# GpSimd's scatters spread out and tied to a tile's finish, and the last ranking one beat sooner, in a cross-attention block with a routed feed-forward layer

## The chip, the cores and the metric

One core of one Trainium2 chip. Its engines are TensorE (PE), VectorE (DVE), ScalarE (ACT), GpSimd (POOL) and SyncE (SP, which here only starts transfers). The metric is the device time of one launch in microseconds (us); lower is better.

## The reference, cut to what matters

`x` has 16 batches of 256 rows of 128 features, `ctx` 16 batches of 64 rows. All is float32.

```python
x = x + tanh(g_xattn) * xattn(layernorm(x), ctx)      # 16 heads of 8, masked softmax
h = layernorm(x)
top1 = argmax(softmax(h @ router_w + router_b))       # one of E = 8 experts per row
for i in range(E):
    hh = h @ w1[i] + b1[i]                            # 128 -> 2 * 512
    a, g = split(hh, 2)
    y = (a * sigmoid(g)) @ w2[i] + b2[i]              # 512 -> 128
    out = out + where(top1 == i, y, 0)
x = x + tanh(g_ffn) * out
```

## The kernel before, in words

Everything is written out by hand, engine by engine: each engine has a fixed list of instructions and waits on semaphores for the others. Nothing is reordered by a scheduler.

**The attention stage** runs over the batches b = 0 to 15 (two row tiles of 128 rows each, so 32 row tiles in all). In step i TensorE makes the scores of batch i + 1 while ScalarE takes the exponentials of batch i. TensorE turns the row shifts of a batch (`shifts`, L1299), ScalarE copies them to SBUF (L653), TensorE adds them to the scores (L1221), and only then can the exponentials (L621) start. GpSimd adds the output bias to a batch's rows (`add_bias`, L403), copies queries (`queries`, L409), and works out the scale and shift of the second layer norm (`rstd_2`, L427 to L432), which ScalarE applies (`norm2`, L630).

**Routing.** A row's expert is chosen on VectorE (`choose`, L900 to L913) in six groups of batches. TensorE counts the rows that come before each row of the same expert (`ranks`, L1283 and L1287), VectorE turns this into a row number in a DRAM buffer (`place`, L924 to L932; `pos` is the result), and GpSimd scatters each row tile of 128 rows (its normalized form, its residual and its index, 1056 bytes a row) into the buffer `routed_rows` with an indirect DMA (`scatter`, L416). There are 32 scatters. The first 22 (`ET`) are enough for a first table of 14 (`T1`) expert tiles; the last ten (22 to 31) belong to batches 11 to 15. GpSimd does the first 22 in the attention steps, as many in a step as `room` allows: those of group 3 (18 to 21) in step 14.

**The expert stage** runs over `FT` = 39 tiles of 128 routed rows. For tile t: SP fetches the rows (`fetch`, L340), TensorE turns them (`turn`, L1387), ScalarE copies the result (`rows`, L697), TensorE multiplies with the expert's first matrix (`up`, L1403; the even tiles go to `ps_A`, the odd ones to `ps_B`), ScalarE takes the sigmoid (`gates_of`, L704), VectorE multiplies (`gate`, L1043), TensorE multiplies with the second matrix (`down`, L1418), VectorE adds the residual (`finish`, L1054, which raises `fo_ready`), and GpSimd scatters the tile to the output (`store`, L486). Before that GpSimd has added the second bias to the fetched rows (`residual`, L480). VectorE and ScalarE also copy the next expert's weights (`weights`, L1033 and L690). TensorE's order in a beat is `up(t + 1)`, `turn(t + 2)`, `down(t)`.

The first 14 tiles run from the first table. Meanwhile the rest of the routing is done: VectorE chooses the last group after `finish(3)`, TensorE ranks it in beat 5, VectorE places it after `finish(5)`, SP writes a block of padding rows behind each expert's region (eight DRAM-to-DRAM transfers of 132 KB, L352), GpSimd sends scatters 22 to 25 in the first beats and 26 to 31 in beats 6 to 10, and VectorE makes the second table in three pieces (`tiles_left`, `second_table`, `second_rows`, L1004 to L1021) after `finish(6)`, `finish(7)` and `finish(8)`. SP fetches tile 14 only when all scatters and padding have landed and the second table is there.

## Time and profile before

| | us |
|---|---|
| median of 3 runs | 280.49 (278.85 to 280.64) |
| the profiled execution | 280.14 |
| its span, first to last instruction | 278.0 |

| engine | busy | share of the span |
|---|---|---|
| TensorE, matmuls | 245.6 | 88% |
| VectorE | 209.0 | 75% |
| GpSimd | 158.5 | 57% |
| ScalarE | 156.7 | 56% |

TensorE has 80% of the chain of work that ended last. The profiled execution lies 0.35 us under the median, and 2.14 us of it lie outside the span. Times below are counted from the start of the span. In the rows, "idle before <- releaser" is the time in which the engine did nothing before that instruction, and what ended it; "remote" and "another core or an unknown queue" stand where the profile finds no event that fits the release.

### The profile page before, as it was taken

To read this page: it belongs to the slowest core of one execution; us is meant where nothing else is said; L and a number is where in the kernel's file an instruction comes from. 1 tells how busy PE (TensorE), PEld (TensorE's weight loads), DVE (VectorE), ACT (ScalarE), POOL (GpSimd) and SP (SyncE) were. 2 spreads that over 40 slices of the span, in tenths; PEclk is the share of its full clock that TensorE was granted. 3 is DMA by queue.
4 is the path that set the end of the run, shared out by engine and by line. 5 is a ranking of instruction groups with operands and counts; after the bars stand their busy time and mean duration, and the time that the engine had idled before them with its cause. 6 is when DMAs were issued, how large, how long until landed. Compare 5 with 4: busy or idle time off the path is not lost.

```text
span 278.0 us, 8458 instructions
## 1 busy us (share of the span) xinstructions
PE 245.6 (88%) x2411; PEld 184.2 (66%) x2411; DVE 209.0 (75%) x608; ACT 156.7 (56%) x436; POOL 158.5 (57%) x254
## 2 busy tenths in 40 slices
PE   3979999999999989989599899399979999999950
PEld 2554445555555555544248899299979999999940
DVE  6988998898989879879649489276757777776720
ACT  5487978777566566545086765256434444444410
POOL 6505426259677585384833775826863645577740
PEclk9999999999999999999989999889999999999995
DMA  6999930000111010021244401535442222100000
GB/s 177 258 298 368 348 114 4 2 1 2 41 40 41 22 60 23 19 80 41 78 103 136 119 28 44 175 90 138 119 111 66 64 84 58 47 21 22 22 5 0
DMA packets 22412, 24.13 MB, mean 87 GB/s; under 512 B 3728, under 2 KB 19539, under 8 KB 22241
## 3 DMA queue, kind: packets, MB, share of 16 engines
q1 hardware_dynamic: 18880, 17.05, 21.7%
q0 software_dynamic: 2784, 6.43, 6.5%
q8 instruction: 21, 0.34, 0.5%
q10 hardware_dynamic: 704, 0.13, 0.2%
q14 instruction: 23, 0.18, 0.2%
HBM read 16.23 MB, written 8.91 MB: 90 GB/s over the span
## 4 chain that ended last, share of the span: by engine, by line
PE 80%; ACT 5%; issue 5%; another core or an unknown queue 3%; DVE 2%; POOL 2%; ACTq 1%; POOLq 0%
PE ps_B L1403 12%; PE ps_A L1403 12%; PE ps_O L1238 11%; PE ps_O L1418 6%; PE ps_B L1204 5%; PE ps_Y L1418 5%; PE ps_A L1176 4%; PE ps_Y L1249 3%; PE ps_B L1269 3%; PE ps_B L1212 3%; PE ps_B L1163 2%; PE ps_A L1181 2%; PE ps_B L1221 2%; PE ps_B L1140 1%
## 5 line engine op out<-in xcount | busy, mean ns | idle before, releaser
L486 POOL DMA_INDIRECT out_dram<-sb_early,sb_k x39 | 39.3, 1008 | 32.8 <-DVE sb_early L1054 30.2
L416 POOL DMA_INDIRECT routed_rows<-sb_xr,sb_pos x32 | 33.1, 1034 | 25.1 <-DVE sb_pos L932 9.2
L1403 PE MATMUL ps_B<-sb_early 128*128 128x128 f32 x304 | 38.8, 282 | 7.4 <-ACT sb_early L697 7.3
L870 DVE TENSOR_REDUCE sb_shift<-ps_A 128x16 bf16<-128x1024 f32 x32 | 39.0, 1218 | 6.3 <-PE ps_A L1181 5.7
L1403 PEld LDWEIGHTS ps_B<-sb_early 128*128 128x128 f32 x304 | 36.8, 198 | 8.1 <-ACT sb_early L697 8.1
L1403 PE MATMUL ps_A<-sb_early 128*128 128x128 f32 x320 | 39.1, 275 | 0.4 <-ACT sb_early L697 0.4
L621 ACT ACTIVATE sb_pT<-ps_B 128x512 f32<-128x512 f32 x64 | 33.0, 603 | 10.0 <-PE ps_B L1221 10.0
L1403 PEld LDWEIGHTS ps_A<-sb_early 128*128 128x128 f32 x320 | 37.3, 192 | 0.7 <-ACT sb_early L697 0.7
L1043 DVE SCALAR_TENSOR_TENSOR sb_qT<-ps_A,sb_b1T,sb_qT 128x128 f32<-128x128 f32 x80 | 22.5, 344 | 19.9 <-ACT sb_qT L704 12.6
L704 ACT ACTIVATE sb_qT<-ps_A,sb_b1T 128x128 f32<-128x128 f32 x80 | 22.8, 367 | 24.9 <-PE ps_A L1403 22.5
L704 ACT ACTIVATE sb_qT<-ps_B,sb_b1T 128x128 f32<-128x128 f32 x76 | 21.8, 368 | 23.7 <-PE ps_B L1403 21.1
L1043 DVE SCALAR_TENSOR_TENSOR sb_qT<-ps_B,sb_b1T,sb_qT 128x128 f32<-128x128 f32 x76 | 21.4, 344 | 14.7 <-ACT sb_qT L704 12.3
L859 DVE RECIPROCAL sb_inv<-ps_O 128x128 f32<-128x128 f32 x32 | 30.3, 946 | 1.8 <-PE ps_O L1238 1.7
L480 POOL TENSOR_TENSOR sb_k<-sb_k,sb_b_g 128x128 f32<-128x128 f32 x39 | 25.7, 660 | 8.7 <-DMA sb_k<-routed_rows 6.7
L1033 DVE COPY sb_early<-sb_w 128x1024 f32 (+1 forms) x39 | 24.8, 637 | 2.5 <-issue 2.5
L1418 PE MATMUL ps_O<-sb_w,sb_qT 128*128 x160 | 21.2, 276 | 0.0
L630 ACT ACTIVATE sb_xr<-sb_xr,sb_nmr,sb_rstd 128x128 f32<-128x128 f32 x32 | 14.1, 487 | 12.0 <-POOL sb_nmr L432 12.0
L1418 PE MATMUL ps_Y<-sb_w,sb_qT 128*128 x152 | 20.3, 277 | 0.0
L1418 PEld LDWEIGHTS ps_O<-sb_w,sb_qT 128*128 128x128 f32 x160 | 19.4, 192 | 0.0
L1204 PE MATMUL ps_B<-sb_qT,sb_k 32*128 32x256 f32 x256 | 18.3, 400 | 1.0 <-issue 1.0
L1418 PEld LDWEIGHTS ps_Y<-sb_w,sb_qT 128*128 128x128 f32 x152 | 18.5, 192 | 0.0
L427 POOL TENSOR_SCALAR sb_neg<-sb_mv 128x2 f32<-128x2 f32 x16 | 3.8, 234 | 25.4 <-DVE sb_mv L891 22.9
(183 smaller groups left out, 464.1 us busy)
## 6 DMA issues: line engine op xcount, KB each, us to landing
sb_k<-routed_rows SPq DMA_DIRECT2D x39, 132.0 KB, 2.0
sb_w<-in_L_ffn_w_dram SPq DMA_DIRECT2D x4, 1024.0 KB, 11.2
sb_w<-in_L_ffn_w_dram SPq DMA_DIRECT2D x4, 512.0 KB, 10.2
sb_xr<-in_x_dram SPq DMA_DIRECT2D x3, 512.0 KB, 7.0
routed_rows<-routed_rows SPq DMA_DIRECT2D x8, 132.0 KB
routed_rows<-sb_pad_rows SPq DMA_DIRECT2D x7, 132.0 KB, 5.7
out_dram<-sb_early,sb_k POOLq DMA_INDIRECT x39, 2.5
sb_ctx_sb<-in_ctx_dram SPq DMA_DIRECT2D x2, 256.0 KB, 4.0
```

The source lines that it names most:

```text
L416: pool.indirect_dma_start(routed[:, :], bass.IndirectOffsetOnAxis(ap=pos[:, t:t + 1], axis=0), xr[:, t, :], None, bounds_check=ROWS - 1, o ...
L480: pool.tensor_tensor(fr[:, k, 0:D], fr[:, k, 0:D], b2_g[:, bass.ds(e, 1), :].rearrange("p o d -> p (o d)"), ALU.add).then_inc(res_ready, 1)
L486: pool.indirect_dma_start(out_rows, bass.IndirectOffsetOnAxis(ap=fr[:, k, 2 * D:2 * D + 1].bitcast(I32), axis=0), fo[:, k, :], None, bound ...
L621: act.activation(pT[:, g, :, :].rearrange("p a s -> p (a s)"), psB[g][:, :], ACT.Exp, scale=SCALE)\
L704: act.activation(sig[:, k, f * P:(f + 1) * P], gate_bank(k)[:, f * P:(f + 1) * P], ACT.Sigmoid, bias=b1T[:, bass.ds(e, 1), FB + f:FB + f + ...
L859: dve.reciprocal(inv[:, q], psO[:, S + t * P:S + (t + 1) * P]).then_inc(inv_ready, 1)
L870: dve.tensor_reduce(shift_parts[:, t, :, 0:HG], psA[:, :].rearrange("p (g h k) -> p g h k", g=G, k=C), AX.X, ALU.max).then_inc(a_max, 1)
L1043: dve.scalar_tensor_tensor(out=hid[:, k, f * P:(f + 1) * P], in0=up_bank(k)[:, f * P:(f + 1) * P], scalar=b1T[:, bass.ds(e, 1), f:f + 1].r ...
L1204: pe.matmul(psB[g][:, k * S:(k + 1) * S], k4[r, b, 2 * k:2 * k + 2, :].rearrange("p h k -> p (h k)"), qT[r, b, :], start=(k == 0), stop=Fa ...
L1238: last = pe.matmul(psO[SLOT * g:SLOT * g + SLOT, c * S:(c + 1) * S], kept, pT[:, g, k, :], start=(k == 0), stop=(k == 1), tile_position=(0 ...
L1403: last = pe.matmul((up_bank, gate_bank)[c](k)[:, f * P:(f + 1) * P], w_1s[:, k, o:o + P], fxT[:, k, :], start=True, stop=True)
L1418: last = pe.matmul((psO, psY)[k][:, 0:D], hid[:, k, f * P:(f + 1) * P], w_2[:, bass.ds(e, 1), f:f + 1, :], start=(f == 0), stop=(f == FB - 1))
```

## The change

1. GpSimd, attention steps: in a step that may scatter several tiles, the first one (the first two in step 14) goes out, then come the bias addition and the copy of queries, and then the other scatters. Before, all scatters came first. In step 14 `rstd_2` moves behind all of it.
2. GpSimd, expert stage: each beat t > 0 now waits for `finish(t - 1)` ahead of its scatter or store. The six late scatters (26 to 31) go out one a beat in beats 5 to 10; before, two in beat 6 and one in each of beats 7 to 10, with no wait for a finish. The stores of tiles 4 and on come correspondingly later.
3. VectorE: the expert numbers of tiles 1 and 2 are read from the table after the first weight copies and not ahead of them; the last `place` stands after `finish(4)`, the pieces of the second table after `finish(5)`, `finish(6)` and `finish(7)`.
4. TensorE: the last `ranks` stands after `down(4)`, ahead of `up(6)`; before, after `turn(7)`.

```diff
@@ GpSimd, attention steps @@
+                for k in range(2 if i == B - 2 else 1):
+                    if sent < ready and room:
+                        scatter(sent)
+                        sent += 1
+                        room -= 1
+                if i in RSTD_AT:
+                    rstd(RSTD_AT[i])
+                if has(i + 1):
+                    add_bias(i + 1)
+                if streamed(i + 3):
+                    queries(i + 3)
                 while sent < ready and room:
                     scatter(sent)
                     sent += 1
                     room -= 1
                 if i == B - 2:
                     rstd_2(i - 1)
-                if i in RSTD_AT:
-                    rstd(RSTD_AT[i])
-                if has(i + 1):
-                    add_bias(i + 1)
-                if streamed(i + 3):
-                    queries(i + 3)
@@ GpSimd, expert stage @@
                 if t + 2 < FT:
                     residual(t + 2)
+                if t > 0:
+                    pool.wait_ge(fo_ready[(t - 1) % NR], (t - 1) // NR + 1)
                 if t == 0:
                     scatter(ET + 2)
                     scatter(ET + 3)
-                elif 6 <= t < 11:
-                    for k in range(2 if t == 6 else 1):
-                        scatter(late)
-                        late += 1
+                elif 5 <= t < 11:
+                    scatter(late)
+                    late += 1
                 else:
                     store(kept)
@@ VectorE @@
-            e_0, e_1, e_2 = expert(0), expert(1), expert(2)
+            e_0 = expert(0)
             weights(0, e_0)
             choose(LAST_GROUP - 1)
+            e_1 = expert(1)
             weights(1, e_1)
             invert(B - 1)
             place(LAST_GROUP - 1)
             gate(0, e_0)
+            e_2 = expert(2)
             weights(2, e_2)
...
-                if t == 5:
+                if t == 4:
                     place(LAST_GROUP)
                     dve.wait_ge(region_ready, LAST_GROUP + 1)
                     dve.tensor_copy(pad_i[:, :], region0[0:1, :]).then_inc(pad_ready, 1)
+                if t == 5:
+                    tiles_left()
                 if t == 6:
-                    tiles_left()
+                    second_table()
                 if t == 7:
-                    second_table()
-                if t == 8:
                     second_rows()
                     dve.wait_ge(table_ready, 2)
@@ TensorE @@
-                if t == 5:
-                    ranks(LAST_GROUP)
                 if t == T1:
                     pe.wait_ge(table_ready, 2)
                 down(t)
+                if t == 4:
+                    ranks(LAST_GROUP)
```

GpSimd's list in attention steps 13 and 14 (L416 are scatters 16 to 21, L403 the bias additions, L427 and on `rstd_2`). Before:

```order
L416 DMA routed_rows<-sb_xr,sb_pos 34688x264 x2
L403 TENSOR_TENSOR sb_xr<-sb_xr,sb_bo_g 128x2x128
L416 DMA routed_rows<-sb_xr,sb_pos 34688x264 x4
L427 TENSOR_SCALAR sb_neg<-sb_mv 128x2
L428 TENSOR_SCALAR sb_ve<-sb_mv 128x2
```

and now:

```order
L416 DMA routed_rows<-sb_xr,sb_pos 34688x264
L403 TENSOR_TENSOR sb_xr<-sb_xr,sb_bo_g 128x2x128
L416 DMA routed_rows<-sb_xr,sb_pos 34688x264 x3
L403 TENSOR_TENSOR sb_xr<-sb_xr,sb_bo_g 128x2x128
L416 DMA routed_rows<-sb_xr,sb_pos 34688x264 x2
L427 TENSOR_SCALAR sb_neg<-sb_mv 128x2
```

The four scatters of step 14 have a bias addition in their middle, and `rstd_2` stands behind that addition as well.

GpSimd's list in the expert stage where the late scatters begin (L480, now L485, is `residual`, L486, now L491, is `store`). Before, from the store of tile 4 on:

```order
L486 DMA out_dram<-sb_early,sb_k 4096x128 [waits fo_ready4]
...
L480 ISA [waits row_in8]
L480 TENSOR_TENSOR sb_k<-sb_k,sb_b_g 128x128
L416 DMA routed_rows<-sb_xr,sb_pos 34688x264 [waits h_ready,pos_ready] x2
...
L480 ISA [waits row_in9]
L480 TENSOR_TENSOR sb_k<-sb_k,sb_b_g 128x128
L416 DMA routed_rows<-sb_xr,sb_pos 34688x264 [waits h_ready,pos_ready]
```

and now, from the store of tile 3 on:

```order
L491 DMA out_dram<-sb_early,sb_k 4096x128 [waits fo_ready3]
...
L485 ISA [waits row_in7]
L485 TENSOR_TENSOR sb_k<-sb_k,sb_b_g 128x128
L416 DMA routed_rows<-sb_xr,sb_pos 34688x264 [waits h_ready,pos_ready,fo_ready4]
...
L485 ISA [waits row_in8]
L485 TENSOR_TENSOR sb_k<-sb_k,sb_b_g 128x128
L416 DMA routed_rows<-sb_xr,sb_pos 34688x264 [waits h_ready,pos_ready,fo_ready5]
```

The scatters begin one beat earlier, each has a wait for a tile's finish, and the pair is gone.

TensorE's list around the last ranking. Before:

```order
L1418 MATMUL ps_O<-sb_w,sb_qT 128x128
L1403 MATMUL ps_A<-sb_early 128x128 [waits w1_act,hid_ready,w1_ready,fx_ready]
L1403 MATMUL ps_A<-sb_early 128x128 x7
L1387 MATMUL ps_B<-sb_ident,sb_k 128x128 [waits fx_ready,row_in7]
L1283 MATMUL ps_B<-sb_onehot,sb_before 128x48 [waits p_ready,lg_ready,region_ready,onehot_ready]
L1287 MATMUL ps_B<-sb_onehot,sb_ones_b 128x48
```

and now (L1426 is `down`, L1291 and L1295 `ranks`, L1411 `up`, L1395 `turn`):

```order
L1426 MATMUL ps_O<-sb_w,sb_qT 128x128
L1291 MATMUL ps_B<-sb_onehot,sb_before 128x48 [waits p_ready,lg_ready,region_ready,onehot_ready]
L1295 MATMUL ps_B<-sb_onehot,sb_ones_b 128x48
...
L1411 MATMUL ps_A<-sb_early 128x128 [waits w1_act,hid_ready,w1_ready,fx_ready]
L1411 MATMUL ps_A<-sb_early 128x128 x7
L1395 MATMUL ps_B<-sb_ident,sb_k 128x128 [waits fx_ready,row_in7]
```

The ranking stands one `up` and one `turn` earlier.

## Rows read from the trace of the kernel before

**Rows 1.** The chain that ended last, in time: start, us, what; `up(6)`, `up(18)`, `up(38)`.

```profile
166.18 1.79 PE ps_A L1403 x16
...
208.08 1.79 PE ps_A L1403 x16
...
263.86 1.79 PE ps_A L1403 x16
```

**Rows 2.** Timeline, 132 to 138: start, us, engine, line [idle before <- releaser].

```profile
131.99 1.00 POOL L416 DMA_INDIRECT routed_rows<-sb_xr,sb_pos  x1 [2.58 <-DVE sb_pos L932]
...
135.84 0.97 POOL L416 DMA_INDIRECT routed_rows<-sb_xr,sb_pos  x1 [0.31 <-issue]
...
134.84 0.29 PE L1299 MATMUL ps_Y<-sb_identb,sb_shift 128*128 128x128 bf16 x2
...
137.73 0.38 ACT L653 ACTIVATE sb_sm<-ps_Y 128x256 bf16<-128x256 bf16 x1 [4.61 <-remote]
```

**Rows 3.** Timeline, 171 to 180, GpSimd, TensorE, ScalarE and VectorE.

```profile
171.56 1.00 POOL L416 DMA_INDIRECT routed_rows<-sb_xr,sb_pos  x1 [1.15 <-DVE sb_pos L932]
...
179.47 1.00 POOL L416 DMA_INDIRECT routed_rows<-sb_xr,sb_pos  x1 [0.17 <-issue]
...
173.64 0.27 PE L1387 MATMUL ps_B<-sb_ident,sb_k 128*128 128x128 f32 x1
...
179.62 3.39 PE L1403 MATMUL ps_B<-sb_early 128*128 128x128 f32 x16 [4.81 <-ACT sb_early L697]
...
179.29 0.28 ACT L697 ACTIVATE sb_early<-ps_B 128x128 f32<-128x128 f32 x1 [3.38 <-remote]
...
179.43 1.12 DVE L1043 SCALAR_TENSOR_TENSOR sb_qT<-ps_A,sb_b1T,sb_qT 128x128 f32<-128x128 f32 x4 [5.07 <-remote]
```

**Rows 4.** Timeline, 189 to 205, GpSimd, TensorE and ScalarE.

```profile
189.77 0.99 POOL L486 DMA_INDIRECT out_dram<-sb_early,sb_k  x1 [0.30 <-issue]
...
203.37 0.99 POOL L486 DMA_INDIRECT out_dram<-sb_early,sb_k  x1 [0.17 <-issue]
...
202.38 0.27 PE L1387 MATMUL ps_B<-sb_ident,sb_k 128*128 128x128 f32 x1
...
204.69 0.28 ACT L697 ACTIVATE sb_early<-ps_B 128x128 f32<-128x128 f32 x1 [0.99 <-remote]
```

**Rows 5.** SP's issues (start, us from first to last issue), its wait for the table, tile 14's rows on GpSimd.

```profile
139.32 15.96 SPq L340 DMA_DIRECT2D sb_k<-routed_rows  x14
171.62 11.83 SPq L352 DMA_DIRECT2D routed_rows<-routed_rows  x8
186.82 27.65 SPq L340 DMA_DIRECT2D sb_k<-routed_rows  x17
...
SPq L356 <- DVE sb_tile_row L1021: 2.5, 1, 2.5
...
189.03 0.45 POOL L480 TENSOR_TENSOR sb_k<-sb_k,sb_b_g 128x128 f32<-128x128 f32 x1 [6.68 <-DMA sb_k<-routed_rows]
```

**Rows 6.** Timeline, 117 to 121: three scatters in a row, and the shifts of batch 13.

```profile
117.99 1.12 POOL L416 DMA_INDIRECT routed_rows<-sb_xr,sb_pos  x1 [1.55 <-ACT sb_xr L630]
...
118.91 0.28 PE L1299 MATMUL ps_Y<-sb_identb,sb_shift 128*128 128x128 bf16 x2
...
119.32 0.38 ACT L653 ACTIVATE sb_sm<-ps_Y 128x256 bf16<-128x256 bf16 x1 [1.96 <-PE ps_Y L1299]
```

**Rows 7.** Timeline, 138 to 144: the end of `rstd_2(13)`, `norm2(13)`, the first weight copy.

```profile
138.30 0.19 POOL L432 TENSOR_TENSOR sb_nmr<-sb_neg,sb_rstd 128x2 f32<-128x2 f32 x1
...
140.80 0.90 ACT L630 ACTIVATE sb_xr<-sb_xr,sb_nmr,sb_rstd 128x128 f32<-128x128 f32 x2
...
143.72 0.43 DVE L1033 COPY sb_early<-sb_w 128x512 f32 x1 [2.46 <-issue]
```

**Rows 8.** Timeline, 264, VectorE: `finish(36)`.

```profile
264.05 0.34 DVE L1054 SCALAR_TENSOR_TENSOR sb_early<-ps_O,sb_tanh_g,sb_k 128x128 f32<-128x128 f32 x1
```

**Rows 9.** Timeline, 169 to 171, VectorE: the last placing.

```profile
169.98 0.21 DVE L924 TENSOR_TENSOR sb_slot<-ps_B,sb_region 128x48 f32<-128x48 f32 x1
```

## The prediction

> **What bounds the kernel now.** I read the chain of work that ended last, first by engine: TensorE has 80% of it. The same chain in order of time gives the pace of the expert stage. From `up(18)` to `up(38)` it takes 263.86 - 208.08 = 55.78 us for 20 tiles, so 2.79 us a tile with TensorE never idle; the time of a tile there can't be beaten by anything GpSimd does. From `up(6)` to `up(18)` it takes 41.90 us for 12 tiles, where the pace asks for 33.47 [rows 1]. So 8.4 us are lost there. Then I looked in the timelines of the single engines for the place of this loss and for others like it. There are three holes, and each has the same look: TensorE has done its work, the engine that waits for its signal gets it late, and the profile names no releaser.
>
> - First: TensorE turns the shifts of batch 15 at 134.84, 0.29 us long. ScalarE copies them at 137.73, after 4.61 us idle, "remote" [rows 2]. Late by 137.73 - 135.13 = 2.6 us.
> - Second: `turn(9)` ends at 173.91, ScalarE's copy of it starts at 179.29; VectorE's gate starts at 179.43, after 5.07 us idle, also "remote". TensorE waits 4.81 us, and the next `up` takes 3.39 us [rows 3] against 1.79 at full clock [rows 1]: 1.6 us more. Together 6.4 us.
> - Third: `turn(17)` ends at 202.65, its copy starts at 204.69 [rows 4]: late by 2.0, of which the tile loses 1.7, since a normal copy waits a little as well. 6.4 + 1.7 = 8.1, which with the ranking of about 0.2 us in beat 5 accounts for the 8.4.
>
> What they have in common is GpSimd. In the first it sends four indirect DMAs in one row, 1.28 us apart (131.99 to 135.84) [rows 2]. In the second six scatters in 7.9 us, 171.56 to 179.47 [rows 3], while SP sends its eight padding blocks (171.62 on) [rows 5]. In the third nine stores in 13.6 us, 1.7 us apart [rows 4], while SP fetches. The counterparts: with only two scatters out (117.99 and one more of the row of three) the signal of the shifts is late by 119.32 - 119.19 = 0.13 us [rows 6], and where there is one store to each 2.79 us, in the 20 tiles from 208.08 on, nothing is late at all [rows 1]. I take it that TensorE's signals are held up while GpSimd's indirect DMAs come closer than about 2 us for several in a row. The trace shows this together, not as cause and effect.
>
> **Part 1, the scatters of the attention steps.** In step 14 the four scatters get `add_bias` between the second and the third. At 134.84 to 135.13, when TensorE's signal of batch 15 goes out, the third has just begun now; then only two are out, and the addition (about 0.75 us) runs. The nearest case is that of [rows 6], 0.13 us late. I take the hold as gone: ScalarE's copy comes 2.6 us sooner, and with it the exponentials of batch 15. But `norm2(13)`, next on ScalarE at 140.80, needs `rstd_2(13)`. That ends at 138.30 + 0.19 = 138.49 now, and with the addition ahead of it at 138.49 + 0.75 = 139.24. So ScalarE gains only 140.80 - 139.24 = 1.6 us; behind that it is ScalarE's row (`norm2(13)`, weights, table load, `norm2(14)`, the first copy of rows) that lets the expert stage begin. The gain lies between 0 (the hold stays) and 2.6 us (ScalarE catches up the rest from its short waits for TensorE); I take 1.6. If the hold stays, the 0.75 us are hidden: 139.24 is before 140.80. The first scatter of the second pair goes 0.75 us later, so SP's first fetch goes from 139.32 to 140.1, and with the 2.2 us of a fetch (186.82 issued, used at 189.03 [rows 5]) the rows are there at 142.3. The first `turn` is some 2 us behind that. The other steps (6, 9, 12, 13) only swap an addition or a copy that nobody waits for with a scatter: nothing.
>
> **Part 2, the wait for `finish(t - 1)`.** The wait makes one indirect DMA a beat, 2.79 us apart, the spacing that is free of holds. Behind it on GpSimd stand the scatter or store and `residual(t + 3)`; the latter is needed by `finish(t + 3)`, three beats on, and takes 0.45 us [rows 5], so its cover is some 7 us. The stores start later by up to four tiles, and the buffers (14 of them) are refilled late: the store of tile 4 comes in beat 11, and SP fetches tile 18 behind it, some five beats before TensorE turns it. So I cost it at nothing. The second and third holds go in full: 8.1 us. From below: if the padding blocks hold TensorE by themselves, up to 6.4 of it stays.
>
> What is late next is tile 14. Its fetch waits for three things. Now it is the second table that comes last: SP waits 2.5 us for it, and issues at 186.82 [rows 5]. In the new order the table is done a beat sooner and the padding begins sooner (part 3). The last scatter, though, is bound to `finish(9)`. In steady beats a finish starts 0.2 us behind the beginning of the next beat but one's `up` (`finish(36)` at 264.05 [rows 8], `up(38)` at 263.86 [rows 1]). So, counted from the start of `up(11)`, `finish(9)` starts at +0.2, and `turn(14)`, two beats and one `up` of 1.79 us later, at +7.4. The scatter can start some 0.15 us behind the finish, at +0.2 + 0.34 + 0.15 = +0.7. From the last scatter before the first table to SP's first fetch it was 139.32 - 135.84 = 3.48 us [rows 2, 5], which gives +4.2, and the rows are there 2.2 us later, at +6.4. Slack 1.0 us: covered, but not by much. A landing 2 us slower costs 1.0 us, once.
>
> GpSimd's scatters took their 1.00 us in the second hold, with VectorE copying weights in the same beats [rows 3]. The Trainium skill ("SBUF — State Buffer", SBUF: two separate sides) says that GpSimd cannot write the descriptors of its DMAs while VectorE runs a float32 copy from SBUF to SBUF, and gives 3.1 us instead of 0.62 for a DMA in such a collision. The rows don't show such a price; by it the last scatter, released by VectorE's own finish, would be up to 2.5 us late and tile 14 would cost 1.5 us, so 272.2 in place of 270.7.
>
> **Part 3, the last group and the table a beat sooner.** The same instructions on VectorE and TensorE, only moved. `place` starts at 169.98 now, behind `finish(5)` [rows 9]; behind `finish(4)`, which ends near 168.1, it starts 1.9 us sooner. It takes 0.9 us and pushes `gate(6)` and the weights of tile 8 back by that, of which TensorE has near 1.9 us in hand: nothing. TensorE's ranking is 0.2 us in either place. SP's padding starts at some 169.8 in place of 171.62, and its 11.83 us with the landing end near 184, before the last scatter's end. The expert numbers of tiles 1 and 2 leave VectorE's way ahead of the first copy, which now waits 2.46 us for three of them [rows 7]; two thirds, 1.6 us, are gained for VectorE, but the expert stage starts on ScalarE's chain. I take nothing, at most 0.5 us.
>
> **The sum**, against the profiled execution: span 278.0 - 1.6 - 8.1 = 268.3; with the 2.14 us outside the span 270.4; with the 0.35 us by which the profiled execution lies under the median 270.8, rounded to 270.7.
>
> **Rivals.**
>
> 1. The padding is the cause of the second hold. For it: the hold begins 2 us after SP's first padding DMA, and after only two scatters, fewer than in the first hold. Against it: the padding goes on until 183.45, and the signals come at 179.3 [rows 3, 5]. Then 3.2 to 6.4 us stay: 273.9 to 277.1.
> 2. The first hold stays, since four scatters in 5.9 us are still dense: 270.7 + 1.6 = 272.3.
> 3. The holds have nothing to do with GpSimd, but with the place in the program (each engine loading its next piece of code, say), and the change does not do what it is for: 280.5, or 1 us to either side. Against it: in 20 tiles at the spaced pace nothing of the kind shows [rows 1]. The Trainium skill ("Runtime: NRT & Kernel Launch", Instruction fetch mechanics) says that the sequencers stream their code ahead in 16 KiB blocks, mostly hidden; by that such a hold would be rare, which speaks against this rival too.
> 4. Slower: the holds stay, and the fetch of tile 14 now hangs on the last scatter. A hold amid the beats moves `finish(9)` and `turn(14)` alike, so the slack stays 1.0 us. If the last scatter lands 4 us later than I take (held up in its turn), TensorE waits 3.0 us at tile 14 and restarts at the slow clock (1.6 us more, as in the second hold): 280.5 + 4.6 = 285.1; a landing 2.5 us late gives 282.0. It decides from a lateness of 1.0 us. Against it: today's fetches and the first group's scatters landed in the usual time amid dense traffic.
>
> **How the numbers follow.** All three holds go: 0.42, 269.5 to 271.5. Rival 2: 0.14. Rival 1, in part or in full: 0.25. Rival 3: 0.14. Rival 4: 0.05. Faster by over 1% means under 277.7: the forecast, rival 2 and rival 1, together 0.81. Within 1%, which is about what a measurement of this kernel can tell from no change: 0.14. Slower: 0.05. The range that leaves out no more than 2 in 10 reaches from 268 (the 2.6 us of part 1 in full and 0.5 of part 3) to 277.6 (rival 1 in full).
>
> **What would show it.** In the changed kernel's timeline: ScalarE's copy of batch 15's shifts within 0.3 us of TensorE's turn; no "remote" of over 1 us; late scatters 2.8 us apart; TensorE's beats at 2.79 us from tile 8 to 18; `norm2(13)` released by GpSimd; tile 14's rows there within 1 us of its turn. I am wrong if a hold of several microseconds stays while the scatters are spaced (then it is the padding or the place), or if TensorE waits for the fetch of tile 14.

## The result, and the profile after

| | median | lowest to highest | runs |
|---|---|---|---|
| before | 280.65 us | 278.85 to 281.96 | 6 |
| after | 276.71 us | 275.52 to 277.38 | 6 |

The ratio is 0.986, 95% interval 0.982 to 0.990: faster by 1.4%, 3.9 us. The forecast was 270.7, 9.8 us faster. Here and below, executions with a lower granted clock and a time over 1.5% above the kernel's fastest are left out; there are two such of w1 and two of v1. The profiled execution of the changed kernel took 276.95 us, its span is 275.2 us, its mean granted clock 0.989 (before: 278.0 us and 0.976). Line numbers have moved: `up` is L1411 now, `turn` L1395, `down` L1426, ScalarE's gates L710 and its copy of the turned rows L703, VectorE's gate L1049, the store L491, the scatter L416.

First the chain of work that ended last, in order of time (start, us, what), for the pace of `up`: `up(0)`, `up(6)`, `up(13)`, `up(14)`, `up(16)` to `up(20)`, `up(38)`.

```profile
144.57 2.05 PE ps_A L1411 x16
...
164.70 1.89 PE ps_A L1411 x16
...
184.32 1.80 PE ps_B L1411 x16
187.80 1.79 PE ps_A L1411 x16
...
193.38 1.79 PE ps_A L1411 x16
196.85 2.05 PE ps_B L1411 x16
199.90 1.79 PE ps_A L1411 x16
202.69 1.79 PE ps_B L1411 x16
206.29 2.05 PE ps_A L1411 x16
...
261.05 1.79 PE ps_A L1411 x16
```

A "hold" is, as in the prediction, a stretch in which TensorE's signal is late. From `up(6)` to `up(13)` it is 19.62 us for seven tiles, 2.80 a tile: the second hold [rows 3] is gone, and so is the third [rows 4] as one piece. From `up(13)` to `up(14)` it is 3.48 us, 0.69 too much. Then something new: `up(16)` to `up(17)` takes 3.47, `up(17)` to `up(18)` 3.05, the next 2.79, then 3.60 to `up(20)`. Three tiles take 206.29 - 196.85 = 9.44 us where the pace asks for 8.37: 1.07 too much. The same pattern comes six times, with the slow `up` at 196.85, 206.29, 215.75, 225.20, 234.63 and 244.05: 6.4 us in all. Before, from 208.08 on, no tile lost anything [rows 1].

GpSimd's timeline around two of these places (start, us, engine, line; in brackets the idle time before and its releaser):

```profile
189.25 0.99 POOL L491 DMA_INDIRECT out_dram<-sb_early,sb_k  x1 [0.75 <-DVE sb_early L1060]
...
192.51 0.99 POOL L491 DMA_INDIRECT out_dram<-sb_early,sb_k  x1 [1.77 <-DVE sb_early L1060]
193.81 1.28 POOL L491 DMA_INDIRECT out_dram<-sb_early,sb_k  x1 [0.30 <-issue]
...
195.74 0.99 POOL L491 DMA_INDIRECT out_dram<-sb_early,sb_k  x1 [0.17 <-issue]
...
198.88 0.99 POOL L491 DMA_INDIRECT out_dram<-sb_early,sb_k  x1 [1.65 <-DVE sb_early L1060]
```

and ScalarE's gates of the same tiles:

```profile
191.63 1.14 ACT L710 ACTIVATE sb_qT<-ps_B,sb_b1T 128x128 f32<-128x128 f32 x4 [1.48 <-PE ps_B L1411]
...
195.48 1.14 ACT L710 ACTIVATE sb_qT<-ps_A,sb_b1T 128x128 f32<-128x128 f32 x4 [2.54 <-PE ps_A L1411]
```

The reader is to see that the stores are one a beat, except where a second one follows at once (192.51 and 193.81, then 195.74). That is the kernel's catch-up: in each third beat `if t % 3 == 2 and ... kept < t` sends a second store. In that beat ScalarE's gate waits 2.54 us in place of 1.48. It starts 1.06 us later after the start of its `up` than in the beats beside it, 0.39 us after the pair's second store ends (195.09) and before the third starts. Behind the gate stands ScalarE's copy of the next tile's rows (196.50, 0.29 us), and the next `up` starts when it is done, at 196.85. That `up` takes 2.05 us in place of 1.79; the granted clock is 1.00 from 194 to 200, so this is not the clock. A group so loses some 0.8 us by the late start of the `up` and 0.26 by its length.

In the kernel before, the stores ran free, and the backlog was gone at 207. But its timeline has such a pair too, in the beat that the same rule picks:

```profile
200.36 0.99 POOL L486 DMA_INDIRECT out_dram<-sb_early,sb_k  x1 [0.16 <-issue]
201.65 1.06 POOL L486 DMA_INDIRECT out_dram<-sb_early,sb_k  x1 [0.30 <-issue]
```

The third hold begins there. ScalarE's gate of that beat, at 202.56, waited 2.24 us, and the copy of rows came 2.04 us after its turn [rows 4]. The six stores before this pair, from 189.77 to 198.24 and 1.6 to 2.0 us apart, made no gate wait over 1.48 us. So the third hold was itself a pair of this rule, and the change turned one into six.

The first hold moved and shrank. Scatters started at 131.27, 132.55, 134.45 and 135.75, with the addition between the second and the third. ScalarE copied the shifts of batch 15 at 136.51, released by TensorE, not 137.73 after a "remote" wait [rows 2]. But VectorE's reciprocal ahead of it started late:

```profile
134.03 0.96 DVE L865 RECIPROCAL sb_inv<-ps_O 128x128 f32<-128x128 f32 x1 [2.25 <-remote]
```

TensorE's products for it ended at 132.38, between the first two scatters (131.27 to 132.25 and 132.55 to 133.53), and VectorE starts on them at 134.03, 0.5 us after the second has ended. TensorE waited 1.46 us ahead of batch 15's scores, before 0.32. So a pair makes a hold in this stage too.

`up(0)` came at 144.57, before at 146.52: 1.95 us gained, 1.6 forecast.

### The profile page after: what moved, and what is told of

Same layout as the page of the kernel before. It is cut to its first block, busy times and chain, and to the rows that moved or that the text cites. A ratio compares the mean times of both kernels' runs of the same rounds, so it can differ in the third digit from the quotient of the medians.

```text
span 275.2 us, 8490 instructions
## 1 busy us (share of the span) xinstructions
PE 245.3 (89%) x2411; PEld 183.3 (67%) x2411; DVE 208.8 (76%) x608; ACT 156.5 (57%) x436; POOL 153.3 (56%) x254
## 4 chain that ended last, share of the span: by engine, by line
PE 79%; issue 6%; DVE 4%; ACT 3%; DMA 2%; POOL 1%; ACTq 0%; SPq 0%; POOLq 0%; DVEq 0%
PE ps_A L1411 13%; PE ps_B L1411 12%; PE ps_O L1246 10%; PE ps_O L1426 6%; PE ps_Y L1426 6%; PE ps_B L1212 6%; PE ps_A L1184 3%; PE ps_B L1277 3%; PE ps_B L1220 3%; PE ps_Y L1257 3%; PE ps_B L1171 2%; PE ps_A L1189 2%; PE ps_B L1229 2%; DMA sb_xr<-in_x_dram 2%; ACT sb_pT L627 2%
## 5 line engine op out<-in xcount | busy, mean ns | idle before, releaser
L491 POOL DMA_INDIRECT out_dram<-sb_early,sb_k x39 | 39.6, 1015 | 37.0 <-DVE sb_early L1060 31.1
L416 POOL DMA_INDIRECT routed_rows<-sb_xr,sb_pos x32 | 33.3, 1039 | 27.2 <-ACT sb_xr L636 7.5
L1411 PE MATMUL ps_A<-sb_early 128*128 128x128 f32 x320 | 39.5, 277 | 2.8 <-issue 2.4
L1411 PE MATMUL ps_B<-sb_early 128*128 128x128 f32 x304 | 37.6, 277 | 3.4 <-issue 2.6
L1411 PEld LDWEIGHTS ps_A<-sb_early 128*128 128x128 f32 x320 | 37.3, 192 | 3.7 <-issue 3.0
L1411 PEld LDWEIGHTS ps_B<-sb_early 128*128 128x128 f32 x304 | 35.4, 192 | 4.5 <-issue 3.3
L710 ACT ACTIVATE sb_qT<-ps_A,sb_b1T 128x128 f32<-128x128 f32 x80 | 22.8, 368 | 26.9 <-PE ps_A L1411 26.9
L710 ACT ACTIVATE sb_qT<-ps_B,sb_b1T 128x128 f32<-128x128 f32 x76 | 21.8, 369 | 26.5 <-PE ps_B L1411 25.8
L1049 DVE SCALAR_TENSOR_TENSOR sb_qT<-ps_A,sb_b1T,sb_qT 128x128 f32<-128x128 f32 x80 | 22.5, 345 | 17.6 <-ACT sb_qT L710 13.1
L1049 DVE SCALAR_TENSOR_TENSOR sb_qT<-ps_B,sb_b1T,sb_qT 128x128 f32<-128x128 f32 x76 | 21.4, 345 | 15.9 <-ACT sb_qT L710 8.1
L485 POOL TENSOR_TENSOR sb_k<-sb_k,sb_b_g 128x128 f32<-128x128 f32 x39 | 19.9, 511 | 4.5 <-DMA sb_k<-routed_rows 2.4
L1426 PE MATMUL ps_O<-sb_w,sb_qT 128*128 x160 | 21.3, 276 | 0.4 <-DVE sb_qT L1049 0.4
L1426 PE MATMUL ps_Y<-sb_w,sb_qT 128*128 x152 | 20.2, 276 | 0.0
L1426 PEld LDWEIGHTS ps_O<-sb_w,sb_qT 128*128 128x128 f32 x160 | 19.4, 192 | 0.7 <-issue 0.7
L1426 PEld LDWEIGHTS ps_Y<-sb_w,sb_qT 128*128 128x128 f32 x152 | 18.5, 192 | 0.0
L427 POOL TENSOR_SCALAR sb_neg<-sb_mv 128x2 f32<-128x2 f32 x16 | 3.7, 234 | 25.0 <-DVE sb_mv L897 23.2
```

The costliest lines, as they stand in the source:

```text
L416: pool.indirect_dma_start(routed[:, :], bass.IndirectOffsetOnAxis(ap=pos[:, t:t + 1], axis=0), xr[:, t, :], None, bounds_check=ROWS - 1, o ...
L491: pool.indirect_dma_start(out_rows, bass.IndirectOffsetOnAxis(ap=fr[:, k, 2 * D:2 * D + 1].bitcast(I32), axis=0), fo[:, k, :], None, bound ...
L710: act.activation(sig[:, k, f * P:(f + 1) * P], gate_bank(k)[:, f * P:(f + 1) * P], ACT.Sigmoid, bias=b1T[:, bass.ds(e, 1), FB + f:FB + f + ...
L1049: dve.scalar_tensor_tensor(out=hid[:, k, f * P:(f + 1) * P], in0=up_bank(k)[:, f * P:(f + 1) * P], scalar=b1T[:, bass.ds(e, 1), f:f + 1].r ...
L1411: last = pe.matmul((up_bank, gate_bank)[c](k)[:, f * P:(f + 1) * P], w_1s[:, k, o:o + P], fxT[:, k, :], start=True, stop=True)
L1426: last = pe.matmul((psO, psY)[k][:, 0:D], hid[:, k, f * P:(f + 1) * P], w_2[:, bass.ds(e, 1), f:f + 1, :], start=(f == 0), stop=(f == FB - 1))
```

## The experiments

Eighteen runs on five chips, called B to F here; A is the chip of the result, which the record doesn't name. Each ran beside the kernel before on its own chip. The kernel before itself has a trace on A and C alone; elsewhere the last column goes by the traces of the kernels that ran there.

| chip | kernel before there | runs of before | holds in the traces |
|---|---|---|---|
| A | 280.65 | 6 | yes |
| B | 268.34 | 25 | none |
| C | 268.88 | 29 | none |
| D | 268.38 | 18 | none |
| E | 283.47 | 7 | yes |
| F | 282.86 | 7 | yes |

So the first finding was not asked for: the same kernel takes 268 us on B, C and D and 281 to 283 on A, E and F. B to F were used on one occasion each, so the chip and what else went on at that time can't be told apart. Ratios below are to the kernel before on the same chip, with their 95% interval.

### Chip B

**x1_no_pairs.** The changed kernel without the second store of each third beat; what is left over is stored after the last tile.

```diff
-                    if t % 3 == 2 and t > 11 and kept < t:
-                        store(kept)
-                        kept += 1
-            store(FT - 1)
+            while kept < FT:
+                store(kept)
+                kept += 1
```

> The changed kernel with never two stores in one beat; the nine stores that it is behind go out in a row after the last tile. Pair theory (TensorE's signals are held when two indirect DMAs follow each other 1.3 us apart and a third soon after): every beat from tile 18 to 38 is 2.79 us, up(18) to up(38) takes 55.8 us and not the 62.2 of the changed kernel, and no TensorE signal is over 0.3 us late; the whole time is about 270.5 plus 9 to 12 us of stores at the end, so 279 to 283. Rival (the lateness belongs to the place in the program, or to the wait for a finish): the beats of tiles 20, 23, 26, 29, 32 and 35 stay about 1.07 us longer.

Measured: 276.10 us (two executions), ratio 1.025 (1.016 to 1.034). With no hold there is nothing to save, and the leftover shows: seven stores (not nine, as expected) after the last paced one at 256.70, 1.28 us apart, the last at 265.62. The catch-up can't simply be dropped.

**x2_addition_in_pair.** The changed kernel with one of the additions that GpSimd makes anyway (`residual`) put between the two stores of a pair.

```diff
+                    if added < FT:
+                        residual(added)
+                        added += 1
                     store(kept)
```

> The changed kernel with the next tile's residual addition between the two stores of a pair, so that they start 1.65 us apart and not 1.3. If it is the missing gap between two indirect DMAs: the six late beats go, 276.7 - 6.4 = 270.3. If it is three indirect DMAs within 3.3 us whatever stands between: 276 to 277, as the changed kernel.

Measured: 270.35 us, ratio 1.004 (1.000 to 1.008). That this is the 270.3 of the expectation is an accident: the chip has no holds that could have gone. Nor is the spacing the 1.65 us that was meant. In the trace the stores start at 192.29, 194.50 and 195.79: the addition parts the two stores of the beat, and is then missing ahead of the next beat's store, which follows 1.29 us behind. The pair is moved.

**x3_stores_unpaced.** The changed kernel with the wait for `finish(t - 1)` only in beats 1 to 10: `if 0 < t < 11:`.

> The changed kernel without the wait for a finish from beat 11 on; the late scatters stay paced. Pair theory: GpSimd catches up in one stretch after tile 14's rows are there (nine stores 1.65 us apart), which costs one hold of 0 to 2.5 us as before, and from then on one store a beat and no late beats: 270.5 to 273. If the lateness belongs to the number of stores that are caught up, whenever: 276 to 277.

Measured: 270.42 us, ratio 1.003 (0.999 to 1.007).

**x4_before_scatters_paced.** The kernel before, with that wait in beats 7 to 10 alone, so that four of the late scatters come one a beat.

```diff
+                if 6 < t < 11:
+                    pool.wait_ge(fo_ready[(t - 1) % NR], (t - 1) // NR + 1)
```

> The kernel before with one edit: the late scatters of beats 7 to 10 wait for the finish of the tile before (the pair in beat 6 stays). If the crowd of scatters is the cause of the 6.4 us hold at tile 9: 280.65 - 6.4 to 280.65 - 4.5 = 274.2 to 276.2. If the eight padding blocks are: the hold stays, 280 to 281.

Measured: 269.38 us, ratio 1.002 (0.999 to 1.006). The pair of scatters in beat 6 stays. None of the four says anything of the holds, since chip B has none.

### Chip C

**y1_before_again.** The kernel before, unchanged, for its trace on another chip.

> The kernel before, unchanged, for its trace on the chip of this batch. In the first four experiments the kernel before took 268.3 us beside them, and 280.65 beside the changed kernel. If the holds of TensorE's signals are a matter of the chip or of what runs beside it: where it takes near 268 its trace has no signal over 0.3 us late, where it takes 280 it has the three holds.

Measured: 269.4 us, span 267.2, granted clock 0.983. Its timeline at the place of the second hold, GpSimd, then ScalarE:

```profile
170.13 0.98 POOL L416 DMA_INDIRECT routed_rows<-sb_xr,sb_pos  x1 [0.30 <-issue]
...
171.77 1.00 POOL L416 DMA_INDIRECT routed_rows<-sb_xr,sb_pos  x1 [0.17 <-issue]
...
173.71 1.00 POOL L416 DMA_INDIRECT routed_rows<-sb_xr,sb_pos  x1 [0.16 <-issue]
...
175.37 1.27 POOL L416 DMA_INDIRECT routed_rows<-sb_xr,sb_pos  x1 [0.17 <-issue]
...
175.91 1.14 ACT L704 ACTIVATE sb_qT<-ps_A,sb_b1T 128x128 f32<-128x128 f32 x4 [0.63 <-PE ps_A L1403]
...
178.69 1.14 ACT L704 ACTIVATE sb_qT<-ps_B,sb_b1T 128x128 f32<-128x128 f32 x4 [0.62 <-PE ps_B L1403]
```

The six scatters come in 8.5 us (168.83 to 177.31), in [rows 3] in 7.9, and ScalarE's gates start 0.6 us after it is free, 2.8 us apart, with no "remote". `up(0)` starts at 143.78 and `up(38)` at 253.12; on chip A it was 146.52 and 263.86 [rows 1]. The differences, 2.7 and then 8.0 more, are close to the first hold's 2.6 and the 8.1 of the other two, as the prediction had sized them. For the other two this is good evidence, from one trace on each chip. For the first it is in part luck: on C the granted clock was 0.52 from 129 to 132, on A 1.00, so the two stages differ in more than the hold.

TensorE's signals were also on time amid scatters 1.3 us apart. The first group's scatters start at 130.32, 131.63, 132.91 and 134.19, TensorE's work ends at 132.93 and at 133.47, and VectorE and ScalarE start on it at 133.00 and 133.51.

**y2_after_again.** The changed kernel, unchanged.

> The changed kernel, unchanged, beside the kernel before on the chip of this batch. Pair theory as it was: 268.3 x 0.986 = 264.5. If the holds are absent on this chip (kernel before near 268): no hold to save, so the change is worth its other parts alone, 267 to 270. On a chip with holds (kernel before near 280): 276 to 277.5.

Measured: 269.69 us, ratio 1.001 (0.998 to 1.004). The pairs of stores are there and cost nothing. Only the step to tile 14 is long: `up(13)` at 184.01, `up(14)` at 187.61, 0.81 us too much.

**y3_scatter_order_alone.** The kernel before with part 1 of the change (the order in the attention steps) and nothing else.

> The kernel before with the new order of scatters and additions in the attention steps alone. Without holds on the chip: the kernel before's time within 0.3%. With holds: the first hold goes or shrinks, 1 to 2 us less than the kernel before.

Measured: 270.39 us, ratio 1.005 (1.003 to 1.008), a little over the 0.3% of the expectation. The executions of the kernel before fall in two groups here, 267.7 to 268.9 and 269.5 to 271.2; the ten of this run, 269.8 to 270.8, all lie in the upper one. Differences of half a per cent on the chips without holds may be no more than this.

**y4_after_unpaced.** The changed kernel with no wait for `finish(t - 1)` at all.

> The changed kernel with no wait for a finish at all; the ranking, placing, table and scatters stand where the change put them. Without holds on the chip: within 0.3% of the changed kernel, or faster by what the pace holds up. With holds: the crowd of late scatters is back, 278 to 281.

Measured: 269.49 us, ratio 1.001 (0.998 to 1.004). GpSimd's stores from 187.73 to 205.91 are twelve, 1.65 us apart in the mean (the first two 1.30), and the chain has TensorE at its full pace beside them (5.58 us for two tiles):

```profile
197.32 1.79 PE ps_A L1409 x16
...
202.90 1.79 PE ps_A L1409 x16
```

### Chip D

**z1_part3_alone.** The kernel before with what the prediction calls part 3 (the ranking, the placing and the table a beat sooner), and with the late scatters one a beat from beat 5 but no wait for a finish; attention steps and free-running stores as before.

> The kernel before with part 3 alone: the late scatters from beat 5, one a beat, the last ranking, placing and table a beat sooner, the expert numbers of tiles 1 and 2 later; order of the attention steps and free-running stores as before. Where no hold shows in the trace of the kernel before: this is worth nothing, ratio 1.000 within 0.004. If instead the scatters one a beat by program order do the work of the wait where holds exist (kernel before near 280 us), the second hold is gone or halved here, 274 to 277 us; if the pacing by the wait is what counts, GpSimd still runs ahead and the second hold stays, 279 to 281.

Measured: 269.76 us, ratio 1.003 (1.000 to 1.005): part 3 is worth nothing here, as forecast.

**z2_last_scatters_looser.** The changed kernel, with a looser wait in beats 7 to 10.

```diff
                 if t > 0:
-                    pool.wait_ge(fo_ready[(t - 1) % NR], (t - 1) // NR + 1)
+                    u = t - 1 if t < 7 or t > 10 else t - 2
+                    pool.wait_ge(fo_ready[u % NR], u // NR + 1)
```

> The changed kernel, with the wait of beats 7 to 10 for the finish of two tiles back in place of one, so that the last late scatter goes a beat sooner and with it the fetch of tile 14. Theory: the 0.7 to 0.8 us that TensorE loses between tile 13 and tile 14 come from the fetch that hangs on that scatter, and go: 0.7 us less than the changed kernel on the same chip, the step from tile 13 to 14 at 2.79 us. Rival: they come from VectorE's queue (its gate late for another reason), and the step stays 3.5 us.

Measured: 269.46 us, ratio 1.005 (1.004 to 1.007). The chain shows `up(12)` at 180.76 and `up(14)` at 186.34, which is 5.58 for two tiles: the delay of tile 14 is gone, so it came from the fetch behind the last scatter. The changed kernel was not run on this chip, so the 0.7 us of the expectation can't be seen in the time; the ratio to the kernel before, 1.005, shows no gain.

**z3_addition_in_pair_again** and **z4_before_scatters_paced_again** are x2 and x4 once more.

> The changed kernel with an addition between the two stores of a pair. If this chip shows holds (kernel before near 280 us): the theory that a pair of stores 1.3 us apart delays TensorE's signal by 1.1 us, once in three tiles, six times, gives 276.7 - 6.4 = 270.3, or 273.5 if the addition spaces them only half enough; the rival (the delay of each third tile has to do with something else) gives 276.7. Without holds: 1.00 of the kernel before.

> The kernel before with a wait for the finish of the tile before in beats 7 to 10 alone. If this chip shows holds (kernel before near 280 us): the theory of crowded scatters takes the second hold away, up to 6.4 us, so 274 to 276 us, with the first and the third hold left; the rival (padding or place in the program) leaves it at 280. Without holds: 1.00 of the kernel before.

Measured: 270.34 us, ratio 1.008 (1.007 to 1.010), and 270.82, ratio 1.007 (1.003 to 1.010); 1.00 was expected of both without holds. No holds on D either.

### Chip E

**w1_bursts_of_four.** The changed kernel with its stores from tile 11 to 35 in bursts.

```diff
+                elif t < 11 or t >= 36:
+                    if kept < t:
+                        store(kept)
+                        kept += 1
+                elif t % 4 == 3:
+                    for k in range(5 if t < 20 else 4):
+                        if kept < t:
+                            store(kept)
+                            kept += 1
```

> The changed kernel with its stores in bursts from tile 11 to 35: four (at first five) in a row each fourth beat, none in the beats between, no denser row of indirect DMAs exists in any of the kernels. Theory: a row of indirect DMAs some 1.3 us apart delays TensorE's signals by itself, on any chip, if only it is long enough: then six bursts, each with a hold of 2 to 5 us as in the kernel before on the first chip, 12 us or more over the changed kernel, and 'remote' waits in the trace. Rival: on this chip nothing of the kind happens whatever the spacing; the time is that of the changed kernel within 1 us, up to 2 us more if the additions behind a burst come late to finish.

Measured: 294.15 and 297.88 us, beside 283.47 for the kernel before: 11 to 14 us slower. In the kernel before on chip A there were two holds in the expert stage [rows 3, 4]. Here the list of waits (us in total, times, longest) has:

```profile
DVE sb_qT L1054 <- remote: 32.0, 8, 5.4
ACT sb_early L708 <- remote: 13.0, 7, 3.2
ACT sb_qT L715 <- remote: 6.6, 2, 3.3
```

**w2_spaced_and_looser.** x2 and z2 together in one kernel.

> The changed kernel with an addition between the two stores of a pair and with the late scatters waiting for the finish of two tiles back. If this chip shows holds (kernel before near 280 us): the pair theory and the tile 14 repair give 276.7 - 6.4 - 0.7 = 269.6; the rival (the lengthened third tiles are no matter of pairs) gives 276.0. Without holds: as the kernel before within 0.5 per cent.

Measured: 274.25 us, ratio 0.965 (0.958 to 0.972): the fastest version on a chip with holds, 9.2 us under the kernel before.

**w3_before_scatters_paced_third.** x4 again, here with holds.

> The kernel before with a wait for the finish of the tile before in beats 7 to 10 alone. With holds on this chip (kernel before near 280 us): the theory of crowded scatters gives 274 to 276, the rival (padding or place in the program) 280. Without holds: 1.00 of the kernel before.

Measured: 278.59 us, ratio 0.982 (0.977 to 0.987), 4.9 us faster from one wait in four beats. The time lies between the 274 to 276 of the theory and the 280 of the rival. The trace, of an execution of 280.81 us, explains part of it: at the second hold the beats lose 4.0 us (`up(6)` at 168.69, `up(10)` at 183.84), on chip A before 6.7. The two scatters of beat 6 are not spaced by this wait. With the next they start at 174.07, 175.39 and 177.02, and a hold is left behind them, while behind the fourth and fifth (181.49, 185.32) `up` keeps its 5.58 us for two tiles (183.84 to 189.42). ScalarE's and VectorE's timeline:

```profile
177.24 1.14 ACT L706 ACTIVATE sb_qT<-ps_A,sb_b1T 128x128 f32<-128x128 f32 x4 [2.29 <-remote]
...
178.83 0.28 ACT L699 ACTIVATE sb_early<-ps_B 128x128 f32<-128x128 f32 x1 [0.45 <-remote]
...
178.97 1.13 DVE L1045 SCALAR_TENSOR_TENSOR sb_qT<-ps_A,sb_b1T,sb_qT 128x128 f32<-128x128 f32 x4 [2.08 <-remote]
```

### Chip F

**v1_bursts_again.** w1 once more.

> The kernel with bursts of four stores once more. If this is a chip that shows holds (kernel before over 279 us): again some 16 us over the kernel before, a hold at each burst. If it is one that doesn't (kernel before near 268): the theory that the row of indirect DMAs holds the signals only on some chips gives the changed kernel's time, 268 to 271, and no remote wait of over 1 us even behind rows of five; the rival (every chip has holds, if the row is long enough) gives 275 or more.

Measured: 298.16 us, ratio 1.052 (1.044 to 1.059). One burst in the trace, GpSimd, TensorE and ScalarE:

```profile
203.02 0.99 POOL L491 DMA_INDIRECT out_dram<-sb_early,sb_k  x1 [2.44 <-DVE sb_early L1065]
204.32 1.28 POOL L491 DMA_INDIRECT out_dram<-sb_early,sb_k  x1 [0.30 <-issue]
205.91 0.97 POOL L491 DMA_INDIRECT out_dram<-sb_early,sb_k  x1 [0.30 <-issue]
207.18 0.97 POOL L491 DMA_INDIRECT out_dram<-sb_early,sb_k  x1 [0.30 <-issue]
208.46 0.97 POOL L491 DMA_INDIRECT out_dram<-sb_early,sb_k  x1 [0.30 <-issue]
...
205.51 0.27 PE L1400 MATMUL ps_B<-sb_ident,sb_k 128*128 128x128 f32 x1
...
210.74 1.55 PE L1416 MATMUL ps_A<-sb_early 128*128 128x128 f32 x6 [4.07 <-ACT sb_early L708]
...
206.03 1.14 ACT L715 ACTIVATE sb_qT<-ps_B,sb_b1T 128x128 f32<-128x128 f32 x4 [2.58 <-PE ps_B L1416]
...
210.41 0.28 ACT L708 ACTIVATE sb_early<-ps_B 128x128 f32<-128x128 f32 x1 [3.25 <-remote]
```

This is the second hold of [rows 3] made to order. The kernel before has its third hold one turn earlier; the bursts from 220.14, 236.41, 250.44 and 264.48 make theirs where it has none. TensorE's turn ends at 205.78, just ahead of the third store of five. ScalarE sees it at 210.41, 4.6 us late and 1.0 us after the last store ends (209.43). The burst before it ends at 192.51, and its held copy starts at 193.29, 0.8 us behind. From there to tile 36 no signal is late by over 0.5 us except in a burst.

**v2_after_once_more.** The changed kernel, on the same chip.

> The changed kernel, unchanged. With holds: 0.985 of the kernel before, each third tile about 1 us longer from tile 16 on, and 2 to 3 us over the version with spaced pairs of the same call. Without: 1.00 of the kernel before.

Measured: 278.93 us, ratio 0.986 (0.981 to 0.991), as on chip A. The pairs' pattern is there again: `up(16)` 193.12, `up(17)` 196.68, `up(20)` 206.13, 9.45 for three tiles.

**v3_spaced_and_looser_again.** w2, on the same chip.

> The changed kernel with an addition between the stores of a pair and looser last scatters. With holds: 0.965 of the kernel before, third tiles longer by 0.2 to 0.4 us in place of 1.07. Without: 1.00 to 1.005 of the kernel before.

Measured: 274.22 us, ratio 0.967 (0.961 to 0.972), 4.7 us under the changed kernel beside it. The chain from `up(16)` on:

```profile
195.99 1.79 PE ps_A L1416 x16
198.78 1.79 PE ps_B L1416 x16
201.87 2.05 PE ps_A L1416 x16
204.92 1.79 PE ps_B L1416 x16
...
259.10 1.79 PE ps_A L1416 x16
```

From `up(14)` to `up(38)` (190.40 to 259.10) it takes 68.70 us; v2 takes 73.58 (187.54 to 261.12); the pace asks for 66.96. With the addition in the pair 1.7 us are lost, without it 6.6. So 4.9 us of the pairs' price are gone, on one chip. What is left comes at three places (`up` at 201.87, 219.26, 236.52), some 0.6 us each. GpSimd's timeline shows what sets them apart, at the first of them and at the group behind it:

```profile
197.40 0.99 POOL L491 DMA_INDIRECT out_dram<-sb_early,sb_k  x1 [0.16 <-DVE sb_early L1065]
198.70 1.06 POOL L491 DMA_INDIRECT out_dram<-sb_early,sb_k  x1 [0.30 <-issue]
200.70 0.99 POOL L491 DMA_INDIRECT out_dram<-sb_early,sb_k  x1 [0.45 <-issue]
...
203.90 0.99 POOL L491 DMA_INDIRECT out_dram<-sb_early,sb_k  x1 [1.71 <-DVE sb_early L1065]
205.55 1.26 POOL L491 DMA_INDIRECT out_dram<-sb_early,sb_k  x1 [0.17 <-issue]
207.11 0.97 POOL L491 DMA_INDIRECT out_dram<-sb_early,sb_k  x1 [0.30 <-issue]
```

Of the six groups three still have two stores 1.30 us apart (from 197.40, 214.79 and 232.02), since the addition that parts a pair is missing ahead of the next store, as in x2. These three lose time. The three whose stores are 1.56 us apart and more (from 203.90, 221.28 and 238.62) lose none.

The looser wait costs on this chip what it gives. Tile 14, 0.80 us late in v2, is on time (`up(13)` at 187.61, `up(14)` at 190.40). But four scatters come 1.7 to 1.8 us apart again (169.95 to 175.21), and `up(9)` starts at 176.19 after `up(8)` at 172.87, which with its own 2.05 us in place of 1.79 costs 0.79 us.

v3 also starts its expert stage late, `up(0)` at 146.67, v2 at 144.22. That needn't be its edits: w1 and v1 are the same kernel, and start at 144.83 (on E) and 146.80 (on F). The table of windows has the reason (us, busy time of PE, PEld, DVE, ACT, POOL, PEclk, DMA share, GB/s), of w1:

```profile
137.00:141.00 4.00, 2.89 (x33) 1.60 (x37) 2.58 (x12) 3.30 (x7) 2.75 (x8) 1.00 0.19 61
```

and of v1:

```profile
137.00:141.00 4.00, 3.28 (x17) 1.70 (x17) 2.09 (x10) 2.97 (x7) 1.35 (x5) 0.50 0.23 67
```

Full clock in the one, the lower of the two levels (1.2 GHz) in the other. In v1 and v3 TensorE had waited 1.53 us ahead of batch 15's scores, in w1 and v2, which kept their clock, 0.83; the changed kernel on A kept its clock after 1.46. The start of the expert stage so differs by 2 us between two traces of one kernel, and the 1.6 us forecast for part 1 can't be told from that by one trace.

## Why the prediction was right or wrong

**Right: what the holds are.** The prediction took it from coincidence that GpSimd's indirect DMAs, close together, keep TensorE's signals from the engines that wait. w1 and v1 show it as cause on the chips with holds: bursts put at chosen places make holds there, of the same look and size. w3 takes part of one away with one wait. The rival of the place in the program has fallen with this. So has the rival of the padding, as far as a hold needs none: in v1 SP sends the last padding block by 180 us, and the holds come until 282. Whether the padding adds something in the second hold wasn't tried apart.

**Wrong: how close is too close.** "Closer than about 2 us for several in a row" is not what the rows say. In the kernel before, six stores 1.6 to 2.0 us apart (189.77 to 198.24) held nothing, and the hold came with the pair 1.29 us apart at 200.36. The second hold, too, has a pair at its head (171.56 and 172.87). In the prediction's own counterpart [rows 6], "with only two scatters out", only one was: ScalarE starts at 119.32, the second scatter at 119.42. So that row said nothing of a pair.

**Right: the sizes.** 2.6 and 8.1 us of holds; chip C, without any, is faster by 2.7 and 8.0 at the same places. `up(0)` came 1.95 us sooner against 1.6, but here luck had a part. The first hold did not go: the pair at its head left a TensorE wait 1.1 us longer than before. And `norm2(13)`, at 139.36 in place of 140.80, was not held by GpSimd, whose `rstd_2(13)` ended at 138.53 and not at 139.24; it followed ScalarE's exponentials, which came 1.44 us sooner (137.43 in place of 138.87). These are one trace each; see the spread of `up(0)` under v3. The late scatters at one a beat took the second hold away in full: `up(6)` to `up(13)` at 2.80 a tile.

**Wrong: "The wait makes one indirect DMA a beat, 2.79 us apart, the spacing that is free of holds ... So I cost it at nothing."** This is the step of the prediction that failed: a wait put at 0 us cost 6.4. It failed where it passed from the wait to the spacing. The wait delays the stores, as the prediction itself said, "by up to four tiles", and the loop has a rule that catches up whatever is behind: two stores in each third beat. The wait holds both back until the same finish and then frees both at once, 1.3 us apart, with a third 1.9 us later. Six such groups cost 1.07 us each, 6.4 in all. v3 beside v2 confirms 4.9 of it: it is gone where additions between the stores widen or move the pairs, and the three pairs that v3 still has are the places where it still loses. On C the same pairs cost nothing (y2). In the kernel before, GpSimd ran free and the backlog was gone at 207, so the rule made two pairs only: one 1.56 us apart (from 193.07), which cost nothing, and the one at 200.36, the third hold, 1.7 us. The working should have written down the order of stores beat by beat, with the backlog, until it was gone.

**Wrong by a little: tile 14.** "Slack 1.0 us: covered, but not by much." It was not covered: 0.69 us lost on A, 0.81 on C. Most of it is one term, the 0.15 us from a finish to GpSimd's DMA behind it. In the trace the last scatter starts at 180.42, 0.81 us after `finish(9)` ends (179.61), and the rows are used at 185.89, 7.1 us after the start of `up(11)` in place of 6.4. The row shows GpSimd's addition waiting for the rows of the fetch:

```profile
185.89 0.45 POOL L485 TENSOR_TENSOR sb_k<-sb_k,sb_b_g 128x128 f32<-128x128 f32 x1 [1.62 <-DMA sb_k<-routed_rows]
186.70 0.99 POOL L491 DMA_INDIRECT out_dram<-sb_early,sb_k  x1 [0.36 <-issue]
```

z2 shows the cause, since the loss goes when the last scatters go a beat sooner; by which wait of TensorE it comes about, the rows don't show, since its `turn(14)` follows `up(13)` without a gap (185.95). The prediction's rule from the Trainium skill ("SBUF — State Buffer", SBUF: two separate sides), 3.1 us for an indirect DMA beside VectorE's copies, isn't borne out in size: GpSimd's 39 stores took 1.015 us in the mean and 1.28 at most (1.53 in any run), while VectorE copied weights in every beat. In direction it is: the six stores of over 1.1 us all ran beside such a copy.

**Right: part 3 at nothing.** z1, on a chip without holds: ratio 1.003 (1.000 to 1.005).

**The sum.** Forecast span 268.3. (The working adds up to 270.8 us for the time, not 270.7.) `up(0)` was 0.4 us sooner than forecast, 20.13 us to `up(6)` in place of 19.66 (+0.5), the pairs +6.4, tile 14 +0.7: 275.5, and the profiled span was 275.2. Of the rivals none was the one that happened: the holds neither stayed nor went, they came back in small pieces at a rate that the change itself set. That the measured 276.7 lies within 268 to 277.6 is luck: the upper end was there for the padding, rival 1, and not for this.

**What the prediction couldn't see.** On chips B, C and D the change gains nothing (ratio 1.001, 0.998 to 1.004, on C), because there is nothing to gain: no hold in any trace, whatever the spacing. One trace from one chip can't tell which part of it belongs to the kernel and which to the chip or the moment.

**Open.** Why TensorE's signals are held on A, E and F and not on B, C and D. The kernels, their instructions and the durations of GpSimd's indirect DMAs are the same (1.00 us). Nothing in the profile names what differs. Bursts of five weren't run on a chip without holds, so it isn't shown that those are immune to them; what stands for it is y1, with signals on time amid four scatters 1.3 us apart, y2, with six pairs that cost nothing, and y4, with twelve stores at 1.65 us. Nor was the changed kernel run with its pairs truly removed on a chip with holds, so what the wait by itself would give there isn't known.

## What to carry to other kernels

Where a wait is put in front of work that has a catch-up rule, write out the backlog beat by beat: a gate that releases two waiting things together turns an even stream into pairs. Spread DMAs by putting other work of the same engine between them, and look at the trace for where the gap then closes: here the addition opened one gap and closed the next. On the chips with holds the addition in the pair and the looser wait took another 1.7% (278.93 to 274.22) where the change as it stands had given 1.4%; on those without, the addition's version was 0.4 and 0.8% over the kernel before, which is to be weighed. And time a kernel on more than one chip before tuning away a wait whose releaser the profile can't name.

## What the runs showed of the hardware

- The same program took 268.3 to 268.9 us on B, C and D and 280.7 to 283.5 on A, E and F, a difference of 4.4% and more. Between A and C, whose traces were laid side by side, nearly all of it lies in late signals of TensorE to ScalarE and VectorE.
- On A, E and F, two of GpSimd's indirect DMAs 1.3 us apart delayed TensorE's signal by 0.6 to 1.4 us (after, v2, v3), and every such pair amid the beats did so. In bursts of five or four at that spacing a turn was seen 2.4 to 4.6 us after its end, in nine of twelve bursts 0.7 to 1.0 us after the last store had ended (w1, v1).
- At 1.6 to 2.0 us apart it went both ways: nothing for six stores (before, 189.77 to 198.24) and for three rows of three (v3), but 0.9 us for four scatters (v3, 169.95 to 175.21) and 0.6 to 0.7 us amid eight stores (w3, 194.47 to 206.63). At 2.8 us apart nothing was late.
- An indirect DMA of GpSimd took 0.99 us, and up to 1.28 (after) or 1.53 (x4) when it ran beside one of VectorE's weight copies.
- One kernel began its expert stage 2.0 us apart on two chips (w1, v1), where TensorE's granted clock was 1.00 on one and 0.50 on the other for 4 us.
